# Graph attention stack: probabilities normalised by a pair of heads, turned on VectorE in 32x32 blocks and by two DMAs instead of on TensorE

## What is computed

```
q, k, v = heads(x @ Wq + bq), heads(x @ Wk + bk), heads(x @ Wv + bv)
scores  = einsum('bhqd,bhkd->bhqk', q, k) / sqrt(64)
probs   = softmax(scores + where(adj, 0, -9e15)[:, None], axis=-1)
ctx     = einsum('bhqk,bhkd->bhqd', probs, v)
x       = layernorm(x + ctx @ Wf + bf)
```

## Time and profile before

| | |
|---|---|
| median of 3 runs | 2952.93 us |
| profiled execution, span from first to last instruction | 2950.5 us |
| TensorE matmul busy | 2901.4 us (98%) |
| VectorE busy | 2593.1 us (88%) |
| ScalarE busy | 2428.1 us (82%) |
| GpSimd busy | 1269.5 us (43%) |
| granted TensorE clock, mean | 0.998 |
| DMA, mean | 67 GB/s |

### The profile page before, as it was taken

The page is one execution under the profiler, slowest core; times in us unless marked ns, Lnnn a source line. Parts: engine busy times, 40 slices in busy tenths (PEclk is TensorE's granted clock), DMA queues, the critical chain, the costliest instruction groups (busy, mean ns, idle before and its releaser), DMA issues. The chain is left out here.

```text
span 2950.5 us, 72423 instructions
## 1 busy us (share of the span) xinstructions
PE 2901.4 (98%) x22432; PEld 2635.8 (89%) x22432; DVE 2593.1 (88%) x8649; ACT 2428.1 (82%) x6888; POOL 1269.5 (43%) x1262
## 2 busy tenths in 40 slices
PE   8999999999999999999999999999999999999998
PEld 7888888888889999999999999999999999999997
DVE  6999899999888888888888888888888888888887
ACT  7999999999987777777777777777777777777775
POOL 3777776766643343332332333433323323223233
PEclk9999999999999999999999999999999999999999
DMA  2111111010123222223223222222232222222321
GB/s 91 36 36 36 36 36 36 31 36 31 36 73 110 73 77 77 75 74 81 72 77 109 78 77 75 74 78 74 75 80 77 78 73 77 77 75 75 81 72 55
DMA packets 153211, 198.76 MB, mean 67 GB/s; under 512 B 48896, under 2 KB 115328, under 8 KB 152448
## 3 DMA queue, kind: packets, MB, share of 16 engines
q1 hardware_dynamic: 152832, 194.13, 24.0%
HBM read 68.24 MB, written 50.33 MB: 40 GB/s over the span
## 5 line engine op out<-in xcount | busy, mean ns | idle before, releaser
L501 POOL TENSOR_TENSOR residual<-x,br 128x384 f32<-128x384 f32 x192 | 189.6, 1008 | 1329.4 <-DVE mix L1031 1316.2
L727 ACT ACTIVATE probs<-logits,nmax 128x256 f32<-128x256 f32 x1152 | 574.0, 502 | 111.0 <-DVE nmax L1001 104.1
L78 PE MATMUL pj<-xt_hi,w_lo 128*128 128x256 f32 x1728 | 506.9, 293 | 0.0
L80 PE MATMUL pj<-xt_hi,w_hi 128*128 128x256 f32 x1728 | 480.9, 278 | 0.0
L79 PE MATMUL pj<-xt_lo,w_hi 128*128 128x256 f32 x1728 | 480.8, 278 | 0.0
L1001 DVE CUSTOM_DVE_ANT_0 logits<-s,mask 128x256 f32<-128x256 f32 x1152 | 432.5, 419 | 5.8
L1022 DVE TENSOR_SCALAR probs<-probs,recs 128x256 f32<-128x256 f32 x1152 | 398.3, 387 | 20.4
L598 ACT ACTIVATE g_exps<-g_v,g_nmax 128x256 f32<-128x256 f32 x768 | 385.1, 514 | 2.5 <-DVE g_nmax L907 0.4
L712 ACT ACTIVATE split<-pj,bc 128x256 fp32r<-128x256 f32 x576 | 241.9, 472 | 158.9 <-PE pj L80 158.9
L720 ACT ACTIVATE stack<-split 64x512 fp32r<-64x512 f32 x576 | 361.9, 628 | 8.7
L78 PEld LDWEIGHTS pj<-xt_hi,w_lo 128*128 128x128 f32 x1728 | 324.2, 188 | 49.2 <-issue 36.6
(11 more groups left out here) (122 smaller groups left out, 8094.3 us busy)
## 6 DMA issues: line engine op xcount, KB each, us to landing
stack<-split SPq DMA_DIRECT2D x576, 128.0 KB, 2.3
y<-out SPq DMA_DIRECT2D x128, 384.0 KB, 2.7
x<-y SPq DMA_DIRECT2D x96, 384.0 KB, 3.1
x<-x SPq DMA_DIRECT2D x32, 384.0 KB, 3.1
adj<-adj SPq DMA_DIRECT2D x128, 64.0 KB, 3.0
w_whole<-att_w SPq DMA_DIRECT2D x3, 2304.0 KB, 11.5
g_w_stage<-gat_w SPq DMA_DIRECT2D x2, 576.0 KB, 5.9
br<-att_b_row SPq DMA_DIRECT2D x3, 192.0 KB, 6.1
```

What stands on the lines that cost most here:

```text
L78: pe.matmul(out, a[1], b[0], start=first, stop=False)
L80: return pe.matmul(out, a[0], b[0], start=False, stop=last)
L727: last = act.activation(probs[:, (HEADS * u + h) % 4, t, :], logits[:, h % 2, t, :], ACT.Exp, scale=-1.0, bias=nmax[:, u, h, t:t + 1], acc ...
```

## The change

TensorE no longer turns the probabilities, and ScalarE and VectorE no longer copy them out of PSUM. Per pair of heads VectorE takes both reciprocals in one instruction (`invert`), multiplies both heads by them in one tensor_tensor of 128x1024 with a broadcast operand (`normalise`), and turns them in 32x32 blocks by two transposes of 128x512 (`turn`). Their source steps over every fourth element, so that a block holds keys four apart. SyncE writes the 512 KB to DRAM (`lay`) and, when it has landed, reads it back with blocks and partitions exchanged (`fetch`). The contexts read that tile. The contexts of `prev` come after its neighbour's second q, k product instead of after the first scores. The second `add_back` and the `statistics` of a sample move to the start of the next slot (sample `old`), and the layer norm with them, ahead of the mask on GpSimd. The projections rotate over three banks, and contexts use half of the banks freed by the turned probabilities. ScalarE's work on the third chunk of q and k and its last exponentials move from the next slot into their own. The order of the crossing is adapted in the same way.

```
             def lay(half, u, c):
+                b = turn_buffer(u, c)                      # (DC * u + c) % 2
+                held(sp, turned, turns(half, u, c), passed)
+                sp.wait_ge(fetched[c], fetches(half, u) - 16)
+                sp.dma_start(turned_dram[c].rearrange("b (r k) n -> (b r) (k n)", k=BLOCKS),
+                             turned_sb[b][:, :, :].rearrange("p k n -> p (k n)")).then_inc(laid[b], 16)
             def fetch(half, u, c):
+                sp.wait_ge(laid[turn_buffer(u, c)], landings(half, u, c))
+                held(sp, contexts, at(DC, half, u, c + 1 - DC), passed)
+                sp.dma_start(pt_sb[:, c, :, :], turned_dram[c].rearrange("b p n -> p b n")).then_inc(fetched[c], 16)
             def sample(half, u, stored_pair, loaded_pair):
+                cur = before((half, u))                    # the sample in front
                 move(half, u, 0)
+                lay(*cur, 0)
+                move(half, u, 1)
+                fetch(*cur, 0)
                 store(half - 2 + u, stored_pair, 1 - u)
-                move(half, u, 1)
+                lay(*cur, 1)
+                fetch(*cur, 1)
+                lay(*cur, 2)
                 move(half, u, 2)
+                fetch(*cur, 2)
                 load_again(half, u, loaded_pair)
...
 VectorE
-            def normalise(half, u, h):
-                dve.reciprocal(recs[:, u, h, :], sums[:, u, h, :]).then_inc(inverted, 1)
-                dve.wait_ge(inverted, at(HEADS, half, u, h + 1))
-                for t in range(NT):
-                    last = dve.tensor_scalar(probs[...t], probs[...t], recs[:, u, h, t:t + 1], None, ALU.mult)
+            def invert(half, u, c):
+                dve.wait_ge(exped, at(HEADS, half, u, 2 * c + 2))
+                dve.reciprocal(recs[:, u, 2 * c:2 * c + 2, :], sums[:, u, 2 * c:2 * c + 2, :]).then_inc(inverted, 1)
+            def normalise(half, u, c):
+                dve.wait_ge(inverted, turns(half, u, c))
+                dve.tensor_tensor(probs[:, heads, :, :]..., probs[:, heads, :, :]...,
+                                  recs[...].unsqueeze(2).to_broadcast([P, 2 * NT, N]), ALU.mult).then_inc(normed, 1)
+            def turn(half, u, c):
+                dve.wait_ge(normed, turns(half, u, c))
+                dve.wait_ge(laid[b], landings(half, u, c) - 16)
+                for kt in range(NT):
+                    last = dve.transpose(
+                        turned_sb[b][:, :, :].rearrange("p k (z h q) -> p k z h q", z=NT, h=2 * NT)[:, :, kt],
+                        probs[:, 2 * b:2 * b + 2, :, kt * P:(kt + 1) * P].rearrange("p h t (r k) -> p k (h t) r", k=BLOCKS))
+                last.then_inc(turned, 1)
             def slot(cur, nxt, prev, ...):                 # the order after, whole
+                old = before(prev)
+                add_back(*old, 1)
                 low_xt(*nxt, 0); low_xt(*nxt, 1)
                 mask_and_max(*cur, 0); mask_and_max(*cur, 1)
+                statistics(*old)
+                invert(*cur, 0)
                 mask_and_max(*cur, 2); mask_and_max(*cur, 3)
                 low_qk(*nxt, 0)
+                normalise(*cur, 0); turn(*cur, 0); invert(*cur, 1)
                 low_qk(*nxt, 1)
                 mask_and_max(*cur, 4); mask_and_max(*cur, 5)
                 low_ct(*prev, 0); low_ct(*prev, 1); low_ct(*prev, 2)
+                normalise(*cur, 1); turn(*cur, 1); invert(*cur, 2)
+                normalise(*cur, 2); turn(*cur, 2)
                 low_qk(*nxt, 2)
                 add_back(*prev, 0)
...
 TensorE
             def slot(cur, nxt, prev, ...):
-                pair_of_transposes(*prev, 2)
                 transpose_x(*nxt, 0); transpose_x(*nxt, 1)
                 pair_of_scores(*cur, 0)
-                pair_of_contexts(*prev, 0..2)
                 make_qk(*nxt, 0)
                 pair_of_scores(*cur, 1)
-                make_v(*nxt, 0)
-                pair_of_transposes(*cur, 0)
                 make_qk(*nxt, 1)
+                pair_of_contexts(*prev, 0..2)              # wait for fetched[c]
                 pair_of_scores(*cur, 2)
+                make_v(*nxt, 0)
                 make_v(*nxt, 1)
                 make_qk(*nxt, 2)                           # waits for low_qk 1
                 make_back(*prev, 0)
-                pair_of_transposes(*cur, 1)
                 make_back(*prev, 1)
...
 ScalarE, order after: high_xt 0, 1; exp 0, 1; high_qk 0, own_rows 0; exp 2, 3; high_qk 1, own_rows 1;
   high_ct 0, 1, 2; exp 4, 5; copy_v 0, 1; high_qk 2, own_rows 2
```

More of the change, by code:

```diff
@@ L67, in every_slot_of_all_layers, with before @@
     slot(None, None, (last, 1), here)
+def before(sample):
+    if sample is None or sample == (0, 0):
+        return None
+    half, u = sample
+    return (half, 0) if u else (half - 1, 1)
 def held(eng, sem, value, passed):
@@ L216, in network @@
         scores, maxed, exped = sem("scores"), sem("maxed"), sem("exped")
[L217 to L220, removed]
+        inverted, normed, turned = sem("inverted"), sem("normed"), sem("turned")
+        laid = [sem(f"laid{b}") for b in range(2)]
+        fetched = [sem(f"fetched{c}") for c in range(DC)]
         contexts = sem("contexts")
@@ L375, in samples_of_layer @@
                     sample(begin + last, u, last - 2 + u, 0 if layer + 1 < LAYERS else None)
-            start(sp, *g_stored, *stored, *moved)
+            start(sp, *g_stored, *stored, *moved, *laid, *fetched)
             g_load(0, 0)
@@ L413, in _ @@
             end = LAYERS * HALVES - 1
+            lay(end, 1, 0)
+            fetch(end, 1, 0)
             store(end - 1, HALVES - 2, 1)
+            lay(end, 1, 1)
+            fetch(end, 1, 1)
+            lay(end, 1, 2)
+            fetch(end, 1, 2)
             store(end, HALVES - 1, 0)
@@ L1126, in crossing @@
                 mask_and_max(*first, 1)
-                normalise(*first, 0)
-                normalise(*first, 1)
+                invert(*first, 0)
                 low_qk(*second, 0, 0)
@@ L1142, in crossing @@
                 g_elu_and_gate(*g_odd)
-                odd_pt(*first, 1)
-                normalise(*first, 4)
-                normalise(*first, 5)
+                normalise(*first, 1)
+                turn(*first, 1)
+                invert(*first, 2)
                 low_qk(*second, 2, 0)
+                normalise(*first, 2)
+                turn(*first, 2)
                 g_statistics(*g_odd)
@@ L1385, in make_back @@
                 for c in range(DC):
-                    last = product(pe, bank(u, f"back{t}")[:, 0:D], (ct_hi[u][:, c, rows], ct_lo[u][:, c, rows]), (hi[:, O, c, :], lo[:, O, c, :]),
+                    last = product(pe, bank(half, f"back{t}")[:, 0:D], (ct_hi[u][:, c, rows], ct_lo[u][:, c, rows]), (hi[:, O, c, :], lo[:, O, c, :]),
                                    first=c == 0, last=c == DC - 1)
```

294 lines of the change are left out of this document (144 added, 150 removed).

## The result

The changed kernel takes 3264.07 us (median of 4 runs, 3262.15 to 3264.52) against 2952.8 us (median of 4, 2952.37 to 2953.56): a ratio of 1.105, 95% interval 1.1036 to 1.1067. The forecast was 2887, its range 2850 to 3250. The profiled execution has a span of 3262.7 us.

The account below looks back on a forecast made before the run. TensorE bounded the kernel at 21.89 us a slot; VectorE was to take over at 20.6 plus 0.5 of waits, taken as 21.15. Over 94 slots 70 us go, the ends add 4: 2887 us, range 2850 to 3250.

Parts of the forecast that it names:

- the term "turn": VectorE's six transposes of 128x512 per slot, taken at 0.60 us each: 3.6 us.
- The bounds, 0.53 and 1.14: VectorE's transpose of 128x512: from 0.53 us, as two multiplications, to 1.14 us at twice the time per element.
- the ends: Crossing and tail, outside the regular slots: 2 us more each, 4 us in all.
- kept and invert: VectorE's steps that stay in the slot, 12.71 us, and three reciprocals for pairs, 0.50 us.
- normalise: VectorE's three 128x1024 multiplications per slot, 1.24 us each plus 0.03 for the semaphore: 3.8 us.
- rival 3: No change: VectorE's transposes at 0.70, or normalise slower beside GpSimd, eat the 0.74 us: 2950 us; chance 0.08.
- waits: VectorE's waits in a slot, mainly for low_xt and the first exponentials: 0.5 us.
- the DMAs: lay about 3.3 us, fetch 3.6, DMA share 0.75 to 0.85; not a bound, hidden by about 1 us.
- Rival 2: VectorE's strided transposes take twice as long, 3.2 us more per slot: 3195 us, up to 3350 with the clock; chance 0.34.
- the clock's part: Half clock on TensorE after its stall, first q, k product 1.7 us late: up to 3350 us, left outside the range.
- the gain of 70 us: Slot of 21.15 us against 21.89, 0.74 us less in each of 94 slots.
- The relief of TensorE: 24 transposes of probabilities leave TensorE: 2.59 us less per slot, 19.30 instead of 21.89.

Follow-up runs that it names:

- experiment 1: The changed kernel with transposes reading 32 neighbouring keys instead of every fourth, both DMAs unchanged, so keys and values are wrongly paired: 2982.23 us.
- experiment 2: The changed kernel with its six transposes replaced by two copies, two multiplications by one and two transposes, each with far and near step: 2999.99 us.
- experiment 4: The changed kernel without lay and fetch, contexts made from zeros: 3251.46 us with far keys, 2972.28 us with near keys.
- experiment 3: The changed kernel with 32 transposes of the identity added on TensorE behind the back product, into a PSUM half nobody reads: 3184.03 us.
- experiments 7 and 8: Series on the changed kernel with near keys: normalisation on GpSimd, then third turn, contexts and SyncE's order moved; first 3154.89 us, best 2802.13 us, ratio 0.949.
- experiment 12: The changed kernel with near keys put in order by four fetches, normalisation on GpSimd, third turn behind third low_qk and first add_back: 3062.39 us, ratio 1.038.
- experiment 17: The version at 2802 us with the changed kernel's order of keys (every fourth) and its single fetch back: 2957.15 us, ratio 1.001.
- e14: As experiment 12, with the third move ahead of the second fetches and the third contexts, ct_hi and ct_lo behind v's matmuls: 2959.48 us, ratio 1.003.

## Why the prediction was wrong

**The failed step is the term "turn".** It took "the row of the same size and one input, the copy of 128x512, at 0.60 us; six are 3.6 us". Measured: 1.01 us each, 6.07 in the slot shown. The bounds, 0.53 and 1.14, held it; the choice between them was wrong. The row chosen was like the new instruction in size and inputs and unlike it in the property that no row showed, the 16 bytes between elements; experiment 1 takes that property away and finds 0.62. That 0.60 comes so close to it is luck: the row is a copy out of PSUM, and a copy of the same size of neighbouring elements in SBUF takes 0.33 us in experiment 2, where the near transpose takes 0.64. So the row differed in the memory that it read and in the operation as well, and the two differences happened to cancel. The rule of the Trainium skill, "SBUF — State Buffer", Specifications (TRN2), that 16-byte cachelines want two hits per line agrees with experiments 1 and 2, with 0.71 against 1.05 us. Section 3.8 of its "Vector Engine (DVE) Microarchitecture Reference", one element per cycle whatever the elements' distance, as I had read it, does not: the rate fell by 40%.

**Of the other terms the ends failed too, and the rest was off by little.** In the slot of 25.66 us:
- kept and invert, 13.2 by the sum, are 25.66 less the three terms below, 13.7: the two low_xt cost 1.12 instead of 0.88, and 0.2 is a gap in front of the second head's scores, which TensorE makes at half clock;
- normalise, 3.8: 1.26 + 1.25 + 1.26 = 3.8. Beside GpSimd's work single ones last 1.4 to 1.5 us, as rival 3 allowed, in experiment 1 (2022.28);
- waits, 0.5: 0.47 + 1.66 = 2.1. The 1.66 is new: the scores late by the slow clock;
- the DMAs: lay 2.7 us (3.3 forecast), fetch 4.4 (3.6), share 0.60 (0.75 to 0.85); hidden in the slots, by experiment 4;
- the ends, 4 us by the sum: 19. They hold nearly all of the 13 us that experiment 4 takes off with the DMAs, where the forecast set a lay and a fetch in the tail (6.9) against what they replace and kept 2.

Of the 4.5 us between this slot and the forecast's 21.15 the turns are 2.5 us, the waits 1.6, the rest 0.4.

**Rival 2 was the case that came, by its own mechanism.** Its list without the clock gave 3195 us; experiment 3, with the clock restored, has 3184. That this is so near is partly luck: the rival's turns are 1.14 us, 0.8 us a slot more than the measured ones, which made up for the low_xt, the normalise beside GpSimd and the ends that its sum had too small. Its stall "of some 4 us" is 3.7, the clock behind it 0.50, the first product late and the total "up to 3350": 3264. The half clock lasted 5.8 us and not 3.3, but VectorE had other work meanwhile and waited 1.0 us a slot on average, where the rival had the product 1.7 us late. The range ended at 3250 because the clock's part was cut off as unlikely. It wasn't: given the stall, the late scores came in each of the 40 slots of the list. What was a separate small chance should have been part of the rival, since the prediction had itself named the row that shows it.

**The case beyond the failed term.** Even with the turn at 0.62 us the gain of 70 us doesn't come: 2980 us. With VectorE at 94% every term counts that the sum had too small: 0.25 for low_xt, 0.25 for a normalise beside GpSimd, the waits. 0.74 us of gain in a slot, on an engine with a full list, was inside the error of that list. The relief of TensorE (2.59 us a slot) was real; the version that turned it into 151 us has three things that the change lacks: near reads, the normalisation on an engine with room, and the third pair's lay early and its contexts late (experiments 7 and 8; its turn stands where the changed kernel has it). Near reads alone give 2980 us, near reads and the normalisation moved 3062 (with the third turn late as well), all but the near reads 2957. Near reads and the new places with the normalisation left on VectorE weren't run, so that this third part is needed is not shown.

**What stays open.** The normalisation on GpSimd with nothing else changed was not run, nor experiment 12 with the third turn in its old place, so what the moved lays and contexts give beyond undoing that late turn is not known, but for the 53 us of the third contexts' place. The prices of a 16-byte step differ by form (a copy by 0.55 us, a multiplication by 0.20); why a multiplication pays less wasn't tried. In experiment 17's layout it wasn't tried whether an earlier third normalisation would hide the step altogether.

## What to carry to other kernels

Choose the row for a new instruction by how it walks memory, not only by operation and size; if no row shows the walk, price the change at the far bound too, and give that case the consequences that its own stall brings, the clock among them. When work leaves the bounding engine for one with a tenth of room, the gain is the room, not the work, and errors of a quarter of a microsecond in a list decide its sign. An order of data that some engine has to read with a step was cheapest here in the DMAs that move it anyway; and after each engine's relief look in the waits for a transfer that the slower engine had been hiding, and move both its producer and its consumer.

## What the hardware showed unexpectedly

- The price of float32 elements 16 bytes apart, per engine: VectorE's transpose of 512 from 0.62 to 1.01 us from start to start, its copy from 0.41 to 0.96 long (means of 45: 0.47 and 1.03), its multiplication from 0.42 to 0.62; ScalarE's exponential of 256 from 0.50 to 0.76; TensorE's moving operand of 256 columns from 0.117 to 0.235.
- GpSimd multiplies 128x1024 in 1.90 us, VectorE in 1.22.
- A transfer of 512 KB cut into four by partitions costs SyncE 1.7 to 2.7 us to issue (four at once, e12 and e14) instead of 0.37; with near reads alone that was hidden, 2980 against 2982 us.
- 32 useless transposes in each slot took 80 us off, by way of the clock.
- VectorE copies 128x512 out of PSUM in 0.60 us from start to start and neighbouring elements within SBUF in 0.33; a transpose within SBUF takes 0.62.
